# One sequence of units for all 64 experts, two shared tiles behind the last expert

## What is computed

```python
x = layernorm(x + attention(x))                       # 2048 x 512
scores = softmax(x @ gate_w.T); gates, idx = top_k(scores, 6)
xe = rows of x, gathered for each expert              # 64 x 128 x 512
ye = (silu(xe @ w1.T) * (xe @ w3.T)) @ w2.T           # inner width 352, for each expert
routed = sum over a row's 6 experts of gate * ye
z = (silu(x @ sw1.T) * (x @ sw3.T)) @ sw2.T           # shared part, inner width 704
x = layernorm(x + routed + z)
```

## Time and profile before

| | |
|---|---|
| median of three runs | 2459.25 us |
| the profiled execution's own time | 2464.26 us |
| its span, first to last instruction | 2462.5 us (1.76 us lie around it) |
| PE busy | 2365.0 us, 96% of the span |
| DVE, ACT, POOL busy | 76%, 58%, 18% |
| attention, to the end of its last unit | 0 to 1562.6 us |
| projection, routing, lead | 1567.0 to about 1843 us |
| expert stage, first `y_sb` to last product | 1843.5 to 2423.5 us |
| end: last adds, sums, layernorm, stores | 2423.5 to 2462.5 us |

### The profile page before, as it was taken

One profiled execution on the slowest core, in us unless ns is written; L12 is line 12 of the kernel. 1 busy time (PEld: TensorE's weight loads), 2 busy tenths in 40 slices (PEclk: granted clock), 3 DMA queues, 4 the chain that ended last, 5 costly groups with the idle time before them and its releaser, 6 DMA issues. The chain is left out here.

```text
span 2462.5 us, 40572 instructions
## 1 busy us (share of the span) xinstructions
PE 2365.0 (96%) x13450; PEld 2057.0 (84%) x13450; DVE 1869.7 (76%) x3775; ACT 1429.9 (58%) x3216; POOL 444.1 (18%) x490
## 2 busy tenths in 40 slices
PE   7999999999999999999999999899999999999993
PEld 6888888888888888888887887688889999998892
DVE  4786787687588588578678678688758888887785
ACT  4564565465455456456456456455447777776774
POOL 0011011011011011011011011277521122222221
PEclk9999999999999999999999999999999999999997
DMA  6443443443343453353444435388559999999997
GB/s 237 142 157 104 131 153 116 132 140 125 120 155 96 123 178 101 123 161 114 125 125 134 125 101 183 136 317 315 184 171 306 313 309 314 307 313 292 277 310 206
DMA packets 220960, 459.92 MB, mean 187 GB/s; under 512 B 27657, under 2 KB 77193, under 8 KB 210768
## 3 DMA queue, kind: packets, MB, share of 16 engines
q1 hardware_dynamic: 174736, 302.39, 35.8%
q0 software_dynamic: 37376, 92.02, 15.8%
q10 hardware_dynamic: 8640, 62.92, 7.2%
HBM read 326.86 MB, written 138.99 MB: 189 GB/s over the span
## 5 line engine op out<-in xcount | busy, mean ns | idle before, releaser
L584 ACT ACTIVATE probs<-bank,neg_max 128x512 f32<-128x512 f32 (+3 forms) x640 | 396.8, 628 | 130.6 <-DVE neg_max L712 101.1
L597 ACT ACTIVATE pT_hi<-turned 128x512 fp32r<-128x512 f32 (+3 forms) x516 | 260.9, 522 | 184.1 <-PE turned L885 180.1
L706 DVE TENSOR_REDUCE max_part<-bank 128x1 f32<-128x512 f32 (+2 forms) x576 | 347.5, 619 | 17.9 <-PE bank L869 8.2
L856 PE MATMUL bank<-x_sb,w_hi 128*128 128x512 f32 x992 | 311.7, 396 | 13.2 <-DVE x_sb L672 12.1
L718 DVE TENSOR_TENSOR pT_lo<-turned,pT_hi 128x512 fp32r<-128x512 f32 (+3 forms) x516 | 290.9, 581 | 38.8 <-ACT pT_hi L597 38.7
L869 PE MATMUL bank<-k_hi,q_hi 128*128 128x512 f32 (+2 forms) x640 | 253.5, 396 | 17.7 <-ACT probs L584 16.2
L900 PE MATMUL z_ps<-pT_hi,v_hi 128*128 128x512 f32 (+3 forms) x640 | 250.5, 391 | 4.5 <-DVE pT_lo L718 2.1
L885 PE MATMUL turned<-ident,probs 128*128 128x128 f32 x1680 | 252.8, 273 | 0.4 <-ACT probs L584 0.3
L2024 DVE TENSOR_TENSOR up_lo<-w_raw,up_hi 128x704 fp32r<-128x704 f32 x256 | 217.3, 885 | 40.5 <-ACT up_hi L1510 39.9
L869 PE MATMUL bank<-k_hi,q_lo 128*128 128x512 f32 (+2 forms) x640 | 233.9, 365 | 0.0
L869 PE MATMUL bank<-k_lo,q_hi 128*128 128x512 f32 (+2 forms) x640 | 233.8, 365 | 0.0
(11 more groups left out here) (217 smaller groups left out, 5508.8 us busy)
## 6 DMA issues: line engine op xcount, KB each, us to landing
w_raw<-in_w SPq DMA_DIRECT2D x256, 352.0 KB, 5.6
x_sb<-x_parts ACTq DMA_DIRECT2D x60, 1024.0 KB, 6.9
w_raw<-in_w SPq DMA_DIRECT2D x128, 256.0 KB, 5.7
far_dram<-stage SPq DMA_DIRECT2D x124, 256.0 KB, 3.1
probs<-far_dram POOLq DMA_DIRECT2D x124, 256.0 KB, 3.6
rows_in<-gathered_x SPq DMA_DIRECT2D x64, 263.5 KB, 5.4
spread_sb<-inv_dram POOLq DMA_DIRECT2D x64, 256.0 KB, 4.2
z_dram<-z_sb SPq DMA_DIRECT2D x64, 256.0 KB, 2.3
```

Of the source, the lines that this page charges most:

```text
L584: nc.scalar.activation(probs[:, u % 2, r, kc * CHUNK:kc * CHUNK + used], bank[:, job_at["s", h, c, r, kc] % BANKS, 0:used], ACT.Exp, bias= ...
L597: nc.scalar.activation(turned_parts(0, h, c, j), turned_tile(i, h, c, j), ACT.Copy).then_inc(turn_hi, 1)
L706: nc.vector.reduce_max(max_part[:, row % ROWS, kc:kc + 1], bank[:, job % BANKS, 0:used], axis=AX_X).then_inc(part_done, 1)
L856: mark = nc.tensor.matmul(dst, w_sb[a][:, dt, first:first + DH], x_of(b, dt), start=(dt == 0 and (a, b) == PASSES[0]), stop=(dt == DT - 1 ...
```

## The change

All 64 experts run in one body of 88 units: groups of three experts behind an s unit, each fifth group of four experts, and four s units behind the last expert. The s units among the experts are 20 and not 24. The written-out order of pieces is replaced by one that is computed from a window for each piece; there are still 5 or 6 for most units (7 for four of them, 3 in unit 83, none in the last four). The number of instructions of each product stays.

The buffers of the end are laid out anew: `sums_in` lies over the experts' raw weights and one of their weight buffers (`raw`, `up0`), which the last four units don't use. SP fetches tiles 0 to 13 of the sums once the last expert's add and the shared adds of tiles 12 and 13 have landed, and tiles 14 and 15 each after its own add. DVE and ACT wait for the last product before they write the end's buffers.

At the end of attention the last store of `z_sb` counts on another semaphore, for which only SP waits, in the next block. The zeroing that stood behind that store is issued one unit earlier, that of `sums_dram` in the middle of the last pair.

```diff
@@ rooms
-        ends = [sb("sums_in", [P, TILES, DM], F32, part), sb("yc", [P, TILES, DM], F32, part),
...
+        y_out = sb("yc", [P, TILES, DM], F32, part)
...
+    with ExitStack() as part:
+        end_pad = sb("end_pad", [P, (32768 + 2048 + 8192 + 32768) // 4], F32, part)
+        ends = [sb("sums_in", [P, TILES, DM], F32, part), y_out, *small]
@@ attention, SP
+            zeroed = [[u] for u in range(n_units - 2)] + [[n_units - 2, n_units - 1], []]
...
-                        sp.dma_start(dst, z_sb[:].rearrange("p (t n) -> p t n", n=P)).then_inc(z_out[u % 2], 16)
-                        empty = gathered_x[i * (EXPERTS // PAIRS) + u]
-                        sp.dma_start(empty[:, 0:EMPTY], empty_row[:, 0:EMPTY]).then_inc(zero_out, 16)
-                        sp.dma_start(empty[:, EMPTY:], empty_row[:]).then_inc(zero_out, 16)
+                        final = last and u == n_units - 1
+                        sp.dma_start(dst, z_sb[:].rearrange("p (t n) -> p t n", n=P)
+                                     ).then_inc(begun.wo_in[0] if final else z_out[u % 2], 16)
+                        for e in zeroed[u]:
+                            empty = gathered_x[i * (EXPERTS // PAIRS) + e]
+                            sp.dma_start(empty[:, 0:EMPTY], empty_row[:, 0:EMPTY]).then_inc(zero_out, 16)
+                            sp.dma_start(empty[:, EMPTY:], empty_row[:]).then_inc(zero_out, 16)
+                        if last and u == n_units // 2:
+                            for first in range(0, DM, EMPTY):
+                                sp.dma_start(sums_dram[SEQ:SEQ + P, first:first + EMPTY], empty_row[:, 0:EMPTY]
+                                             ).then_inc(zero_out, 16)
...
-            for first in range(0, DM, EMPTY):
-                sp.dma_start(sums_dram[SEQ:SEQ + P, first:first + EMPTY], empty_row[:, 0:EMPTY]).then_inc(zero_out, 16)
...
-                sp.wait_ge(z_out[n], 8 * n_units * (PAIRS + 1))
+                sp.wait_ge(z_out[n], 8 * n_units * (PAIRS + 1) - 16 * n)
@@ route_and_experts
-    BODIES = 4
+    BODIES = 1
-    PATTERN = "seeseeeseee" * 2
+    PATTERN = ("seee" * 4 + "seeee") * 4 + "ssss"
+    TRAIL = 2
...
+    def window(e, p):
+        at = [u for u, unit in enumerate(UNITS) if unit == ("e", e)][0]
+        back = unit_of["e", e - 2] if e > 1 else -2
+        return (back + 1, at - 1) if p in UP else (back + 2, at)
...
-            share(e, UP, 2, 4) + share(e, DOWN, 0, 1) + share(e + 1, UP, 0, 2),
...
+        due = sum(window(*piece)[1] <= u for piece in open_)
+        pieces_of_step.append(open_[:max(due, 5 if u % 4 else 6)])
@@ POOL
-            tile_after = {1: 0, 7: 1, 12: 2}
+            tiles_after = {}
+            for s in range(NST):
+                before = sum(kind == "e" for kind, _ in UNITS[:unit_of["s", 2 * s + 1]])
+                tiles_after.setdefault(before - 1, []).append(s)
@@ SP, beginning
+            sp.wait_ge(wo_in[0], 32)
@@ SP, end
             for n in range(2):
                 sp.wait_ge(y_stored[n], (16 * NE // 2) * BODIES)
-                sp.wait_ge(ys_stored[n], slot_count(BODIES - 1, 2 - n, 16))
+                last_there = NST - TRAIL - 1 - n
+                sp.wait_ge(ys_stored[tile_slot(last_there)], slot_count(0, last_there, 16))
             for t in range(TILES):
+                if t >= TILES - TRAIL:
+                    sp.wait_ge(ys_stored[tile_slot(t - FIRST)], slot_count(0, t - FIRST, 16))
                 sp.dma_start(sums[:, t], sums_dram[t * P:(t + 1) * P]).then_inc(loaded[t], 16)
@@ ACT, end
+            act.wait_ge(down_ready, after(BODIES, NU, 0))
@@ DVE, end
-                dve.wait_ge(gate_step, i * NE + NE)
-                nc.vector.tensor_scalar(mine[:], mine[:], float(NE), None, ALU.add).then_inc(mine_ready, 1)
...
+            for u in range(NU - 2, NU):
+                shared_result(BODIES, u, True)
```

More of the change, by code:

```diff
@@ L965, in share @@
         return [(e, p) for p in which[a:b]]
-    pieces_of_step = []
-    for e in range(0, NE, 8):
-        pieces_of_step += [
-            share(e, UP, 2, 4) + share(e, DOWN, 0, 1) + share(e + 1, UP, 0, 2),
[L972 to L982, removed]
+    def window(e, p):
+        at = [u for u, unit in enumerate(UNITS) if unit == ("e", e)][0]
+        back = unit_of["e", e - 2] if e > 1 else -2
+        return (back + 1, at - 1) if p in UP else (back + 2, at)
+    EARLY_PIECES = [(0, 0), (0, 1)]
+    left = [(e, p) for e in range(NE) for p in range(NP) if (e, p) not in EARLY_PIECES]
+    pieces_of_step = []
+    for u in range(NU):
+        open_ = sorted((piece for piece in left if window(*piece)[0] <= u), key=lambda piece: (window(*piece)[1], piece[0], piece[1]))
+        due = sum(window(*piece)[1] <= u for piece in open_)
+        pieces_of_step.append(open_[:max(due, 5 if u % 4 else 6)])
+        left = [piece for piece in left if piece not in pieces_of_step[-1]]
+    assert not left and max(len(step) for step in pieces_of_step) <= 7
+    pieces_of_step[-1] = pieces_of_step[-1] + [(e + NE, p) for e, p in EARLY_PIECES]
     pieces = [piece for step in pieces_of_step for piece in step]
@@ L1004, in tile_slot @@
     def tile_slot(s):
-        return s % 2
+        return (FIRST + s) % 2
     def slot_count(i, s, each):
-        if tile_slot(s) == 0:
-            return i * (2 * each) + each * (FIRST // 2 + 1 + s // 2)
-        return i * each + each * (FIRST // 2 + 1)
+        return each * ((FIRST + s) // 2 + 1)
     def tile_count(i, s, less=0):
@@ L1295, in add_rows @@
                     pool.wait_ge(y_stored[(n - 1) % 2], i * (16 * NE // 2) + 16 * ((n - 1) // 2 + 1))
[L1296 to L1299, removed]
+                for s in tiles_after.get(n - 1, ()):
+                    wait_apart(pool, ys_free, ys_stored[tile_slot(s)], slot_count(i, s, 16))
                 wait_apart(pool, waited4, y_read, after(i, NE, n + 1))
@@ L1313, in body @@
                     add_rows(i, n)
-                    if n in tile_after:
-                        add_shared(i, n, tile_after[n])
+                    for s in tiles_after.get(n, ()):
+                        add_shared(i, n, s)
             for i in range(BODIES):
@@ L1412, in _ @@
             load_tile(FIRST, tile_slot(0))
-            tile_step = {unit_of["s", 2] - 2: (1, -1), unit_of["s", 4] - 2: (2, unit_of["s", 1]),
-                         NU - 2: (NST, unit_of["s", 5])}
+            tile_step = {unit_of["s", 2 * s] - 2: (s, unit_of["s", 2 * s - 3] if s > 1 else -1) for s in range(1, NST)}
             for i in range(BODIES):
@@ L1420, in _ @@
                         load_rows(i, UNITS[u + 1][1])
-                    if u in tile_step and not (u == NU - 2 and i == BODIES - 1):
+                    if u in tile_step:
                         s, over = tile_step[u]
                         sp.wait_ge(up_ready, after(i, NU, over + 1))
-                        load_tile(i * NST + (FIRST + s), tile_slot(s % NST))
+                        load_tile(FIRST + s, tile_slot(s))
                     for q in in_step(i, u):
@@ L1573, in body @@
                         turned(i, ("x", 0))
-                    if not (first and u < 2):
-                        result(i, (u - 2) % NU, u < 2)
+                    if u > 1:
+                        result(i, u - 2, False)
                     loads = in_step(i, u)
```

13 lines of the change are left out of this document (7 added, 6 removed).

## The result

The changed kernel took 2485.11 us (median of 5 runs, 2482.04 to 2487.39) against 2461.19 us for the kernel before (5 runs, 2458.58 to 2468.48). The ratio is 1.0091 with a 95% interval of 1.0073 to 1.011: slower by 0.9%. The forecast was 2448 us, with 0.13 on slower, and the time lies outside the range of 2436 to 2473. The profiled execution of the changed kernel took 2487.39 us, its span is 2485.7 us. PE (TensorE) was busy for 2377.9 us where it was 2365.0 before.

The account below looks back on a forecast made before the run. PE sets the pace, with the queue of adds as full; 2464.26 - 15.4 (end) - 3.6 (attention's end) + 8 (adds) = 2453.3 us, less 5.0 for the runs' median: 2448 us, range 2436 to 2473.

Parts of the forecast that it names:

- The end: After PE's last product: DVE's first measuring comes 0.9 us behind it and not 16.3, saving 15.4 us.
- The end of attention: Between attention and next block: the block ends right after its last store, first transfer about 1563.3, 3.6 us earlier.
- The units: Expert stage: PE's work per 16 experts falls from 146.64 to 140.38 us, 548.1 us from first to last expert's copy.
- Splits: DVE's splitting of weight pieces: four units with 7 pieces cost nothing; 4 x 1 us if DVE became the bound.
- The adds: GpSimd's one-at-a-time adds in the expert stage become slower than PE: extra between 0.4 and 15.7 us, taken as +8.
- the two ends (7.72 and 7.93): Assumed us per add: undisturbed bodies' 7.72 and whole stage's mean 7.93, giving PE losses of 10.2 and 25.5 us.
- The rival at 2475 us: Expert stage: adds sharing DMA engines with the weights slow to 8.15 us or more, losing more than is won; chance 0.13.
- its signs: Expert stage: distances between adds over 8.1 us, or PE at half clock in many places.
- the four cases: Adds pace at 7.7 to 7.95 us (0.45); adds at no extra cost (0.25); much slower adds (0.13); ends bring less (0.17).
- the bytes of the earlier trace: Expert stage's DMA traffic, 45.0 to 45.8 MB over 146.64 us, used to argue that adds would not get faster.
- 7.51 us: Expert stage: the distance between adds that PE's 548.1 us would ask for.
- the estimate of 2.6 us: Time of one 256 KB add by the Trainium skill's rule, under which the adds' extra would be nothing.

Follow-up runs that it names:

- experiment 8: Kernel before with only the change at attention's end: 2459.49 us against 2463.77. Separately, changed kernel with up pieces first and all fetches after the last add: 2475.65 us.
- experiment 2: Every second expert's add left out: 2440.45 us in the changed kernel with up pieces put before down pieces, 2484.94 us in the changed kernel with its own order.
- Experiment 3: Kernel before, with one or two down pieces put ahead of the four up pieces in 16 steps: 2474.64 us, ratio 1.0054.
- experiment 5: Changed kernel with up pieces before down pieces, and all four due up pieces, not three, split ahead of the product: 2474.82 us, ratio 1.0043.
- experiment 1: Changed kernel with up pieces put before down pieces due at the same step: 2467.44 us, ratio to the kernel before 1.0016.
- experiment 6: Changed kernel with up pieces first, and shared tiles stored plainly and added on the way into SBUF at the end: 2448.92 us, ratio 0.9947.

## Why the prediction was wrong

**The end** (forecast -15.4 us): right. DVE's first measuring is 0.64 us behind PE's last product (2463.44 against 2462.80), forecast 0.9.

```profile
2462.82 0.69 DVE L2033 COPY ys_sb<-ys_ps 128x512 f32<-128x512 f32 x1 [2.44 <-PE ys_ps L1799]
2463.44 0.69 DVE L2154 BATCH_NORM_STATS2 statsc<-sums_in 128x6 f32<-128x512 f32 x1
```

**The end of attention** (-3.6): right in mechanism, 3.4 us at the seam, in experiment 8 as in the changed kernel (0.95 us from store to next block). The next block's first transfer came at 1565.60 and not at 1563.3 only because this execution's attention ended later.

**The units** (548.1 us from first to last `y_sb` if nothing waits): nearly right, 552.0 in experiment 2.

**Splits** ("Four units have 7 pieces where 6 was the most; ... with 11% free around it: nothing"): this is the step that failed. It priced the number of splits per step and DVE's busy share, and the change had moved their order. In the four steps that it looked at PE waits 2.67 us each, 10.7 us in all, and not nothing or 4 x 1 us; the other 28.3 us lie in 30 steps that it did not look at. DVE's free time did not cover them: it lies ahead of the product `h_sb`, and the late pieces stand behind it. The up buffers of expert e come free only when the up product of e - 2 is through. In a run of three experts that leaves the third one a single step for all four up pieces, in a run of four the last two; that makes 24 steps. The planner's order also makes up pieces late in 10 others. The order written out by hand had them first there (`share(e + 4, UP, 0, 4) + share(e + 3, DOWN, 2, 3)`); the planner sorts what is due by expert, and so puts the older expert's down pieces first. A down piece may be late by most of a step, since the down product follows the up product; an up piece may not. The price was not 0 to 4 us but 44.5 us with half of the adds out (experiment 2), and 17.7 us as long as the adds stand behind it. Experiment 3 gets 12.7 us from the same exchange in 16 steps of the old kernel. The working for it was within reach: an up piece is 0.88 us on DVE and starts 0.80 us behind the one before, and each down piece ahead of four up pieces puts one more of them behind the product.

**The adds** (forecast: the slower side, +8 us): right in mechanism, too small, and hidden in the changed kernel. With the order mended PE's last product comes at 2444.38, which is 603.3 us after the first `y_sb`, 23.3 more than before, where +8 was forecast; 15.2 of them are PE standing still more than before (4.1 for `up_lo`, most of the rest for `h_sb` behind an add) and 8.1 are longer busy time. From one add to the next it was 7.98 us, with 51 of them released by the one before; that is past the dearer of the two ends (7.72 and 7.93) between which I took the middle. It is also the value from which the prediction had itself said that the change would be no gain. So even with a good order the change only breaks even (ratio 1.0016).

**The rivals.** The rival at 2475 us came nearest in time, and its signs were there: distances of 8.19 us and low clocks. It was still the wrong mechanism. In the changed kernel leaving half of the adds out changed nothing. None of the four cases named the splits.

**Two slips in the working** changed nothing: the bytes of the earlier trace rows less 0.8 MB are 315 to 320 GB/s over 140.38 us, and not 318 to 323; and 7.51 us is nearly three times the estimate of 2.6 us, not twice.

Not settled: why the adds stood 7.98 us apart and not 7.7 with the order mended, and why experiment 5 was slower than experiment 1.

## What to carry to other kernels

When a planner takes the place of an order written by hand, put the two lists side by side at the tightest step and find the last item that the pacing engine waits for; the number of items and the engine's busy share don't show it. Two queues that each fall behind don't add: test both alone and together before giving either a price, and expect the second to appear when the first is mended. Where a serialized queue is as full as the pacing engine, take work out of it before making the stage denser.

## What the runs showed of the hardware

- Behind a stall of 1.89 us in dense matmuls the granted clock went from 1.00 to 0.50 some 1 us after the products had resumed, and rows of 0.49 us stand where the shape takes 0.32, for about 3 us. PE's busy time in the stage was 14.6 us longer than in experiment 2, beside 32.0 us more of standing still. Stalls of 1.1 us did not do it, though they recurred in every fourth step: in the first window, with five of them and one of 2.7 us, the clock is 1.00 and PE is busy for 139.82 us, against 139.77 in experiment 2.
- At the end of experiment 6 ten transfers with add of 256 KB were issued close behind each other: the first took 6.9 us to its landing and the tenth 12.6. A plain store of that size behind the ten took 12.70 us, and the last transfer with add, issued when all but one of the others had landed, 5.10 us. The queue ahead of a transfer decided its time more than its kind.
- The chained adds stood 7.98 us apart at 273 to 313 GB/s and held PE up (experiment 1), while at 315 to 319 GB/s, in the first three windows of experiment 6, with fewer transfers chained, PE took 141.8 to 142.4 us for each.
